# Attention on half rows of TensorE, loads on ScalarE's queue, splits on GpSimd

## The reference, cut to what matters

```python
qkv = x @ W_qkv.T + b_qkv            # -> Q, K, V (b, 16 heads, 1024, 8)
scores = einsum('bhqd,bhkd->bhqk', Q, K) / sqrt(8)
attn = softmax(scores + causal, axis=-1)
O = einsum('bhqk,bhkd->bhqd', attn, V)
x = layernorm(x + O @ W_o.T + b_o)
```

## Time and profile before

| what | value |
|---|---|
| median of three runs | 854.17 us |
| the profiled execution | 851.66 us |
| its span | 850.1 us |
| first matmul of the second stage | 61.4 us |
| last output copy of the second stage, start | 541.76 us |
| PE, DVE, ACT, POOL busy, share of the span | 87%, 80%, 67%, 50% |

### The profile page before, as it was taken

One profiled execution on the slowest core, in us unless ns is written; L12 is line 12 of the kernel. 1 busy time (PEld: TensorE's weight loads), 2 busy tenths in 40 slices (PEclk: granted clock), 3 DMA queues, 4 the chain that ended last, 5 costly groups with the idle time before them and its releaser, 6 DMA issues. The chain is left out here.

```text
span 850.1 us, 17568 instructions
## 1 busy us (share of the span) xinstructions
PE 738.5 (87%) x4345; PEld 330.1 (39%) x4345; DVE 684.0 (80%) x2289; ACT 567.2 (67%) x926; POOL 423.6 (50%) x468
## 2 busy tenths in 40 slices
PE   6659899999999999999999998687788788887755
PEld 3332233333333333333333332233546455555345
DVE  5769999898998998989989890166888888888883
ACT  4440267666766676667666778558879798897771
POOL 8655111221122112211221123358999999999984
PEclk9885599999999999999999999997999999999997
DMA  6768535345543553355335330201001101100000
GB/s 174 225 159 200 113 73 120 83 94 125 120 86 84 126 125 80 88 124 126 81 86 123 83 81 23 89 2 52 1 3 36 38 1 38 37 1 13 4 11 25
DMA packets 58955, 67.06 MB, mean 79 GB/s; under 512 B 15488, under 2 KB 33536, under 8 KB 58880
## 3 DMA queue, kind: packets, MB, share of 16 engines
q1 hardware_dynamic: 53120, 62.35, 31.2%
q10 hardware_dynamic: 5184, 2.36, 1.0%
q0 software_dynamic: 576, 1.57, 0.7%
HBM read 46.73 MB, written 19.53 MB: 78 GB/s over the span
## 5 line engine op out<-in xcount | busy, mean ns | idle before, releaser
L698 ACT ACTIVATE probs<-ps 128x384 f32<-128x384 f32 (+2 forms) x384 | 290.9, 809 | 172.8 <-PE ps L752 170.7
L669 POOL TENSOR_SCALAR_AFFINE_SELECT probs<-probs 128x256 f32<-128x256 f32 x256 | 103.0, 407 | 361.4 <-ACT probs L698 359.0
L720 PE MATMUL ps<-Kx,Qx 128*128 128x512 bf16 (+3 forms) x768 | 233.0, 348 | 15.3 <-DVE mx L812 9.7
L808 DVE CUSTOM_DVE_ANT_0 junk<-ps,tri 128x256 bf16<-128x256 f32 (+3 forms) x512 | 228.2, 487 | 22.3 <-PE ps L720 18.8
L752 PE MATMUL ps<-Qa,Ka 128*128 128x512 bf16 (+3 forms) x768 | 180.3, 329 | 3.5 <-ACT probs L698 2.9
L812 DVE TENSOR_REDUCE mx<-ps 128x1 f32<-128x512 f32 x256 | 162.1, 681 | 13.8 <-issue 7.3
L738 PE MATMUL ps<-probs,Vg 128*9 128x512 f32 (+3 forms) x1536 | 153.3, 488 | 0.3 <-POOL probs L669 0.3
L720 PEld LDWEIGHTS ps<-Kx,Qx 128*128 128x128 bf16 x768 | 69.6, 98 | 207.0 <-DVE mx L808 85.8
L967 POOL TENSOR_TENSOR S<-sim 128x1024 f32<-128x1024 f32 x64 | 120.7, 1910 | 10.5 <-ACT sim L1030 5.4
L1219 DVE SCALAR_TENSOR_TENSOR A<-S,T,ps 128x511 f32<-128x511 f32 x128 | 90.1, 741 | 11.3 <-ACT ps L1041 9.4
L1041 ACT ACTIVATE ps<-S,nb 128x512 f32<-128x512 f32 x128 | 82.9, 680 | 11.4 <-DVE A L1219 10.8
(11 more groups left out here) (115 smaller groups left out, 862.6 us busy)
## 6 DMA issues: line engine op xcount, KB each, us to landing
Qx<-q_scr SPq DMA_DIRECT2D x48, 192.0 KB
Kx<-k_scr SPq DMA_DIRECT2D x48, 192.0 KB
Qa<-q_scr SPq DMA_DIRECT2D x48, 192.0 KB
Ka<-k_scr SPq DMA_DIRECT2D x48, 192.0 KB
o_scr<-Os SPq DMA_DIRECT2D x32, 256.0 KB, 2.2
q_scr<-qs SPq DMA_DIRECT2D x34, 128.0 KB, 3.2
k_scr<-qs SPq DMA_DIRECT2D x18, 128.0 KB, 3.1
xin<-in_L_attn_x_dram ACTq DMA_DIRECT2D x8, 256.0 KB, 3.8
```

The lines of the kernel that those rows point to most:

```text
L669: pool.affine_select(out=diag, in_=diag, compare_op=ALU.is_ge, fill=0.0, base=0, pattern=[[0, 2], [1, P]], channel_multiplier=-1).then_inc ...
L698: act.activation(probs[:, k % 2, hh, 0:width], ps[:, bank:bank + 2, :].rearrange("p a c -> p (a c)")[:, 0:width], ACT.Exp, scale=SM_SCALE) ...
L720: pe.matmul(ps[:, X_BANK + f % X_SLOTS, 0:c1 - c0], Qx[:, u, hh, P * i:P * (i + 1)], Kx[:, u, hh, c0:c1], start=True, stop=True).then_inc( ...
L808: dve.tensor_tensor_reduce(out=junk[:, f % 4, 0:w], in0=src, in1=tri[:, CHUNK - w:CHUNK], scale=1.0, scalar=-BIG, op0=ALU.add, op1=ALU.max ...
```

## The change

- The rows of a head are cut from 72 to 64 (the first eight products of parts), so that two heads lie side by side in the halves of the 128 rows: heads `a = 0` on rows 0 to 63, `a = 1` on rows 64 to 127. A max chunk is one matmul on half of the rows, and neighbouring chunks alternate between the halves. The last product of parts and the three rows of the maximum go in operands of their own, `Ql` and `Kl`. A score step is now one key tile of 128 with two heads: four matmuls, two of `Ka`, `Qa` and two of `Kl`, `Ql` that add to them. The number of score steps (24), of exps (24) and of products (12) in a group stays; an exp covers 2 x 512 down to 2 x 128 elements.
- `probs` has four slots of one key tile for two slots of two.
- Transfers: SyncE loads the score operands (10 DMAs and four for `Ql`, `Kl`) and stores the outputs. ScalarE's sequencer stores the maxima (four DMAs, ahead of exp 13 and of the output copy that now stands there too), fetches them as rows (two DMAs) and loads the max operands (10 DMAs), both ahead of exp 18.
- VectorE keeps the join of the maxima and the transpose, five chunks later (`TURN_LATER`); the four operations of the split, and the copy of the values, go to GpSimd, where the split is five operations.
- `AHEAD` is 24, and `GROUP_ORDER` is another.
- In the diff below, the second `split_max` and `group` are GpSimd's, and the loop over `e` with the copy is ScalarE's.
- First stage: loops written out, `qs` with four slots, 48 stores of parts for 64, pads of half the size; the bias loads take four DMAs on ScalarE's queue for one.

```diff
-GROUP_ORDER = "xpxxpxsxxsxxsxxsxppxxsxsxxpxxxsspxxsxsxppxxsxxsxxxxxsspxsxxsxpxxsxsxpxssxxxpsxsxxsxs"
+GROUP_ORDER = "xxsxpxsxxpxxsxxsxppxssxxpxxssxpxsxxsxpxxxsxxsxxsxpxssxxpxxsxpxxsxsxpxsxsxxpxsxsxxsxs"
-COPY_AT = (12, 4)
+COPY_AT = (13, 4)
+M_STORE_AT, M_FETCH_AT, X_LOAD_AT = 13, 18, 18
+            def m_store(eng, g, reg):
+                eng.wait_ge(m_chain, M_STEPS * (g + 1))
+                for b in range(4):
+                    eng.dma_start(m_scr[reg, :, :, b, :].rearrange("n s c r -> (n c) s r"),
+                                  mT[32 * b:32 * (b + 1), :].rearrange("c (s r) -> c s r", s=PARTS)).then_inc(m_stored, 16)
+            def m_fetch(eng, g, u, reg):
+                eng.wait_ge(m_stored, 64 * (g + 1))
+                for a in range(2):
+                    eng.dma_start(Ql[ROWS * a:ROWS * a + PARTS, u, :, :].rearrange("s j t -> s (j t)"),
+                                  m_scr[reg, :, 16 * a:16 * (a + 1)].rearrange("n s c b r -> (n s) (c b r)")).then_inc(
+                        mrow_loaded[u], 16)
...
+            for a in range(2):
+                eng.dma_start(q[0:2 * FULL], qsrc.unsqueeze(0).broadcast_to([2, FULL, PL * SEQ])).then_inc(done, 16)
+                eng.dma_start(q[2 * FULL:ROWS], qsrc[0:ROWS - 2 * FULL]).then_inc(done, 16)
+                for s in range(PARTS):
+                    ksrc = k_scr[g, a, s].rearrange("n d j t -> (n d) (j t)")
+                    times = PARTS if s < PARTS - 1 else PARTS - 1
+                    eng.dma_start(k[FULL * s:FULL * s + DH * times], ksrc.unsqueeze(0).broadcast_to(
+                        [times, DH, PL * SEQ])).then_inc(done, 16)
...
+                    def split_max(g):
...
+                        wait_alone(pool, m_chain, c + 1, pads_made)
+                        pool.tensor_scalar(mneg[:], mm_[:], -1.0, 0.0, ALU.mult, ALU.add)
+                        wait_alone(pool, m_stored, 64 * g, pads_made)
+                        pool.tensor_scalar(msp[:, 0:32], mm_[:], -1.0, 0.0, ALU.mult, ALU.add).then_inc(m_chain, 1)
+                        wait_alone(pool, m_chain, c + 2, pads_made)
+                        pool.tensor_tensor(mr[:], mneg[:], msp[:, 0:32], ALU.subtract).then_inc(m_chain, 1)
+                        wait_alone(pool, m_chain, c + 3, pads_made)
+                        pool.tensor_copy(msp[:, 32:64], mr[:]).then_inc(m_chain, 1)
+                        wait_alone(pool, m_chain, c + 4, pads_made)
+                        pool.tensor_tensor(msp[:, 64:96], mr[:], msp[:, 32:64], ALU.subtract).then_inc(m_chain, 1)
+                    def group(n, u, last):
+                        masks(n, DIAG_TILES[:4])
+                        if not last:
+                            wait_alone(pool, pv_done, PPG * n + PV_START, pads_made)
+                            pool.tensor_copy(Vg[:, 1 - u, :, :, :], vaug[:, bass.ds(n + 1, 1), :, :, :].rearrange(
+                                "p n j h d -> p (n j) h d")).then_inc(v_staged, 1)
+                            split_max(n + 1)
+                        masks(n, DIAG_TILES[4:])
...
                         for e in range(SPG):
...
+                            if e == M_STORE_AT and not (isinstance(n, int) and n + 1 >= GROUPS):
+                                m_store(act, n + 1, bass.ds(n + 1, 1))
+                            if e == M_FETCH_AT and not (isinstance(n, int) and n + 1 >= GROUPS):
+                                m_fetch(act, n + 1, 1 - u, bass.ds(n + 1, 1))
+                            if e == X_LOAD_AT and not (isinstance(n, int) and n + 3 >= GROUPS):
+                                load_next_max(act, n + 3, 1 - u)
                             if e == COPY_AT[0]:
                                 copy_out(n, 0)
...
-                        pe.matmul(ps[:, X_BANK + f % X_SLOTS, 0:c1 - c0], Qx[:, u, hh, P * i:P * (i + 1)],
-                                  Kx[:, u, hh, c0:c1], start=True, stop=True).then_inc(mx_ready, 1)
+                        pe.matmul(ps[:, X_BANK + f % X_SLOTS, 0:c1 - c0], Qx[rows, u, pl, P * i:P * (i + 1)],
+                                  Kx[rows, u, pl, c0:c1], start=True, stop=True).then_inc(mx_ready, 1)
...
+                        for q, k, first in ((Qa, Ka, True), (Ql, Kl, False)):
+                            for a in range(2):
+                                rows = slice(ROWS * a, ROWS * (a + 1))
+                                mm = pe.matmul(ps[:, S_BANK + 2 * (e % 2) + a, 0:w], k[rows, u, pl, P * j:P * (j + 1)],
+                                               q[rows, u, pl, q0:q0 + w], start=first, stop=not first)
...
                             if f + AHEAD == CPG - 1 and last < 2:
-                                split_max(n + 1)
+                                row_max(n + 1)
+                            if f + AHEAD == CPG - 1 + TURN_LATER and last < 2:
+                                turn_max(n + 1)
```

More of the change, by code:

```diff
@@ L24 @@
 PARTS = 3
[L25 to L26 removed]
+PL = GH // 2
+ROWS = P // 2
+FULL = PARTS * DH
 VW = DH + 1
@@ L204, in build @@
         p3_made = sem("p3_made")
-        qk_stored = [sem(f"qk_stored{u}") for u in range(2)]
-        p3_stored = [sem(f"p3_stored{u}") for u in range(2)]
+        qk_stored = [sem(f"qk_stored{u}") for u in range(QS)]
+        p3_stored = [sem(f"p3_stored{u}") for u in range(QS)]
         pads_made = sem("pads_made")
@@ L287, in build @@
         vaug = operands.enter_context(nc.sbuf_tensor("vaug", [P, GROUPS, SEQ // P, GH, VW], F32))
[L288 to L291 removed]
+        qs = operands.enter_context(nc.sbuf_tensor("qs", [P, QS, 2, PARTS, CHUNK], BF16))
+        Qx, Kx, Qa, Ka, Ql, Kl = [operands.enter_context(nc.sbuf_tensor(name, [P, 2, PL, SEQ], BF16))
+                                  for name in ("Qx", "Kx", "Qa", "Ka", "Ql", "Kl")]
@@ L315, in store_parts, with load_last @@
+        def load_last(eng, u, g, done):
+            for a in range(2):
+                for dst, scr in ((Ql, q_scr), (Kl, k_scr)):
+                    eng.dma_start(dst[ROWS * a + PARTS:ROWS * a + PARTS + DH, u, :, :].rearrange("p j t -> p (j t)"),
+                                  scr[g, a, PARTS - 1].rearrange("n d j t -> (n d) (j t)")).then_inc(done, 16)
+        STORES = 4
         def store_parts(sp, b):
@@ L491, in _ @@
                     turn(0, 0)
-                    with pe.Fori(0, BATCH - 1) as b:
+                    for b in range(BATCH - 1):
                         turn(b, 1)
@@ L557, in _ @@
                     copy_turned(0, 1)
-                    with dve.Fori(0, BATCH - 1) as b:
+                    for b in range(BATCH - 1):
                         for u in range(2):
@@ L669, in group, with masks @@
+                    def masks(n, units):
+                        for t in units:
+                            for pl in range(PL):
+                                wait_alone(pool, exp_done, SPG * n + PL * t + pl + 1 + FREE, pads_made)
+                                diag = probs[:, t % PROB_SLOTS, pl:GH:PL, 0:P]
                                 pool.affine_select(out=diag, in_=diag, compare_op=ALU.is_ge, fill=0.0, base=0,
                                                    pattern=[[0, 2], [1, P]], channel_multiplier=-1).then_inc(masked, 1)
-                    with pool.Fori(0, GROUPS) as n:
-                        group(n)
+                    def group(n, u, last):
[6 more added lines that the diff above has]
+                        masks(n, DIAG_TILES[4:])
@@ L675, in _ @@
+                    split_max(0)
+                    with pool.Fori(0, GROUPS // 2 - 1) as i:
+                        for u in range(2):
+                            group(2 * i + u, u, False)
+                    group(GROUPS - 2, 0, False)
+                    group(GROUPS - 1, 1, True)
                 @block.scalar
@@ L703, in _ @@
-                    with act.Fori(1, GROUPS) as n:
-                        group(n)
+                    group(0, 0)
+                    group(1, 1)
+                    with act.Fori(1, GROUPS // 2 - 2) as i:
+                        for u in range(2):
+                            group(2 * i + u, u)
+                    for n in range(GROUPS - 4, GROUPS):
+                        group(n, n % 2)
                     copy_out(GROUPS - 1, 1)
@@ L743, in scores @@
                     def scores(n, u, e, load):
[L744 removed]
+                        t, pl = divmod(e, PL)
+                        half, j, q0, w = KTILES[t]
                         if e == 0:
[L746 to L747 removed]
+                            pe.wait_ge(sop_loaded[u], S_LOADS * 16 * load)
+                            pe.wait_ge(mrow_loaded[u], M_LOADS * 16 * load)
                         pe.wait_ge(exp_done, SPG * n + e + 1)
[L750 to L753 removed]
+                        for q, k, first in ((Qa, Ka, True), (Ql, Kl, False)):
+                            for a in range(2):
+                                rows = slice(ROWS * a, ROWS * (a + 1))
```

(4 more changed lines are left out.)

307 lines of the change are left out of this document (133 added, 174 removed).

## The result

The changed kernel takes **1006.46 us** (median of 4 runs, 1003.16 to 1008.55) against 853.45 for the kernel before: ratio 1.1801, 95% interval 1.1767 to 1.1834. The prediction was 867 us, 812 to 890.

A forecast was written before the change was run, and what follows sets the result against it. The prediction took VectorE, reducing 48 chunks a group, to bound the kernel. From the profiled 851.66 us it summed -18 - 19 + 30 + 26 + 2 - 5.5 = +15.5 to 867 us, range 812 to 890.

The forecast's parts named there:

- The transfers themselves are hidden: Attention's DMA transfers: no cost, since the engines are busy half the time and max operands are needed a group later.
- The block ahead of exp 18: ScalarE's queue: 12 issues, 5.2 us, delay exp 18; VectorE idles 2.0 us more in 13 groups, +26 us.
- The block ahead of exp 13: ScalarE's queue: four issues delay the output copy and product 8; VectorE idles 2.0 us in 15 groups, +30 us.
- Work taken from VectorE: Split and values copy leave VectorE: 1.2 us in each of 15 groups, counted in full, -18 us.
- TensorE on half rows: Score and max matmuls: pairs on different halves run together, so VectorE's waits for TensorE go, -19 us.
- First stage: Stage before the attention: four slots remove ScalarE's store waits; ends 0 and -12 us, together -5.5 us.
- 24 chunks: Six chunks move ahead of the first group; two more exps follow VectorE's last chunk at the end, +2 us.
- GpSimd late with the split: Rival: the split on GpSimd takes 4.8 us, VectorE stands at the transpose, +26 us, 893 us; chance 0.08.
- Halves one after the other: Rival: half-row matmuls don't run together, a score step takes 0.96 us, TensorE bounds, some 930 us; chance 0.04.
- Issues hidden: Rival: ScalarE's transfer issues cost nothing, 811 us, or 839 with half hidden; chance 0.32 for wholly or by half.
- the balance: Rival: the issue blocks on ScalarE's queue cost what the change gains elsewhere, 850 to 858 us; chance 0.12.

The follow-up runs named there:

- e5: Changed kernel with operand loads of 24 or 16 different rows, none repeated, still issued on ScalarE, and six stores of parts for four: 964.8 us, 1.1321.
- e7: Changed kernel with 24-row loads, none repeated; max operands' loads moved to SyncE, maxima's stores and fetches left on ScalarE: 897.6 us, 1.0533.
- e9: e6 with SyncE's order changed: stores and fetch of the maxima first, the max operands' loads behind them: 863.4 us, 1.0141.
- e8: Changed kernel, its own repeated-row loads, with only the max operands' loads moved to SyncE and the maxima left on ScalarE: 958.6 us, 1.1248.
- e1: Changed kernel, its own repeated-row loads, with every transfer of the attention issued by SyncE, loads ahead of the maxima: 1033 us, 1.2115.
- e6: e5's loads without repeated rows, with all transfers of the attention on SyncE, loads ahead of the maxima: 896.4 us, 1.0519.
- e10: Kernel before with only GpSimd's part: split and copy of the values on GpSimd, transpose five chunks later: 841.7 us, 0.9886.
- e15: Kernel before with the attention's sixteen groups written out, no loops: 840.7 us, 0.9862.
- e18: Kernel before with both GpSimd's part (e10) and the groups written out (e15): 842.3 us, 0.9898.
- e17: e16 with the sixteen groups written out, no loops in the attention: 822.8 us, 0.9662.
- e14: e9 with half the loads ahead of the maxima's stores, half between stores and fetch, and 30 chunks in advance for 24: 897.9 us, 1.0518.
- e16: e9 with half the loads ahead of the maxima's stores, half before the fetch, and the first-half output store behind the fetch: 843.9 us, 0.9911.
- e11: Kernel before, loads still on SyncE but issued behind the maxima's store and fetch, so they land at the turn: 873.8 us, 1.0267.
- e2: Kernel before with its six max operand loads moved to ScalarE's queue ahead of exp 18: 886.7 us, 1.0398.

## Why the prediction was wrong

Three steps take off most of the loss: rows not repeated (after to e5, 42 us), the loads off ScalarE (e5 to e7, 67) and the maxima off ScalarE and first in the queue (e7 to e9, 34). The sum had 0, 26 and 30 for them, 87 us too little. e9 is then 12 us above the kernel before, where the sum's other terms had 40.5 below it; that is the other 52.

**The step that failed: "The transfers themselves are hidden: the DMA engines are busy half of the time".** I took the share of before for the change, though the change replaces every load by ones of another shape. Those move the same bytes at 0.2 of the engines, and are under way always. Without repeated rows the loss falls by 42 us (e5), 61 (e8 to e7) or 137 (e1 to e6), by placement.

The Trainium skill (DMA: Bandwidth & Descriptors, Rules for kernel authors) states the mechanism: a transfer whose outermost dimension has c entries, for instance a leading broadcast of c copies, runs on at most c of the 16 engines. Here c is 2 or 3 in eight of ten loads, and 3 of 16 is 0.19; the trace agrees with 0.18 to 0.22. From the shapes in the diff this could have been read ahead of time. The runs change the outermost dimension and the repeated reading of a row together; none separates the two.

**The block ahead of exp 18 (+26).** The mechanism was right, the size was not: 48 us with after's loads, 67 with the 24-row ones. Twelve issues at 0.43 us were taken from plain loads; eight of them repeat rows and take 0.63 to 0.81, and 5.2 us became 8.4. The forecast idle time of VectorE was 2.0 us and the trace has 6.2. Not in the sum at all was what follows: behind the hole TensorE runs at 1.2 GHz for some 6 us. I did not measure that part by itself; as an estimate, 6 us of work at half clock are at most 3 us lost in a group.

**The block ahead of exp 13 (+30).** The mechanism was right: the wait is there, behind product 8. e7 to e9, which takes the maxima off ScalarE and puts them first in SyncE's queue, gives 34 us. That this is so near 30 is partly luck: the trace has 4.0 us of idle time in a group for the 2.0 forecast, and e9's turns are longer.

**Work taken from VectorE (-18).** Measured 10 us (e10), and nothing when the loops are gone (e15 and e18 are equal within their intervals). "This is on the bounding engine, so it counts in full" was a wrong reading of the earlier trace rows. In e18 TensorE is busy 53.3 of 54.5 us and VectorE 48.9; in e17 VectorE has nearly the same work (47.8) in 51.3 us. A group bound by VectorE could not do that, so with the loops gone I take TensorE to set the group; the waits for PSUM banks don't show which of the two does.

**TensorE on half rows (-19).** The pairs run together, 0.44 us a step. From e18 to e17, both written out and with GpSimd's part, it is 842.3 to 822.8, -19.5 us; that takes in the 24 chunks in advance and the first stage, which the runs don't separate. The size agrees by luck; the reason given for it, VectorE's idle time, doesn't.

**First stage (-5.5) and 24 chunks (+2).** The stage itself ends 10 us earlier, more than I had. But the first loads, issued at 44.96, land only at 67.06, and the first join comes 5 us later than before: +5 in place of -5.5. In the kernel after this is the failed step once more, 22 us for these loads where e5's take 12; but e5 brings nothing here, because its additional stores come first. The first scores start 11 us later (110.17 for 98.92); the other 6 us are in part the six more chunks, which the forecast counted as moved, not as added. That more chunks in advance are free did not hold for e14, which lost 39 us by six.

**The rivals.** GpSimd late with the split is wrong: the transpose waits twice, 1.8 us each, for the first and the last group's maxima, and nowhere in the loop. Its five operations with their waits take 1.5 us, not 4.8. Halves one after the other is wrong: 0.44 us a step, not 0.96. Issues hidden, and with it the balance, is wrong by e7 and e9. The steps from after to e17, in the order they were taken: rows not repeated 42, transfers off ScalarE 68, maxima first 33, loads between 5, output store last 15, no loops 21; 184 us in all, of which 153 is the loss.

**What stays open.** Why the turn costs nothing in e10 and 2.9 us in e16, whose VectorE loop has the same steps. e10's instruction queue is all but empty, so I read the turn as a fetch of code that queues with other transfers; that is argued, and no run takes the fetch away by itself. The Trainium skill (Runtime: NRT & Kernel Launch, Instruction fetch mechanics) says that a branch to code outside the engine's current window stalls for a DMA fetch and favours full unrolling; e15 and e17 agree by 12 and 21 us, while e18 gains nothing over e10. That the turn grows with the transfers under way is what e11 shows, 1.8 to 4.1 us. What the half clock costs is open too.

## What to carry to other kernels

When a change alters the shape of a transfer, its old busy share says nothing: look at the outermost dimension of both sides, and read the share beside the bytes, since a low share all the time with long landings is a few engines at work. For each queue write down its order and what each entry waits for: three of the six repairs here were only moves within SyncE's queue. And before counting an engine's saved work in full, take it away in one run: two engines that wait for each other look alike in the waits.

## What the runs showed of the hardware

An issue that repeats source rows takes 0.63 to 0.81 us, a plain one 0.28 to 0.41 (after, 297.95 to 306.4). An output store of 256 KB that lands in 2.3 us (before) or 2.0 (e5) takes 10.0 when loads with repeated rows are under way (after; 5.5 in e1, 12.4 in e8).

A loop's turn costs VectorE more when the DMA engines were busy in the 4 us ahead of it. In the kernel before it is 1.80 to 1.93 us with a share of 0.22 to 0.33, and with the same loop in e11 and e2 3.6 to 5.2 us with a share of 0.78 to 0.80. In the changed loop it is 2.5 to 3.0 us with a share of 0.19 to 0.35 (e16), and 4.1 to 6.2 us with 0.67 to 0.79 (e9). So the share isn't all: the two loops differ at the same share.

TensorE did nothing from about 301.5 to 307.5 in the kernel after; its granted clock fell to 0.50 in that gap, at 303.5, and was back at 1.00 from 314 on, after some 6 us of work.
